# A four-layer graph network on one NeuronCore: narrower destination ranges, another sum over picked neighbours, another plan of picked passes

## The reference

```python
# layer 0: relational messages, weighted by an attention score of source, destination and relation
a   = tanh(relu(sum((x[src] @ A1.T + b1) * (x[dst] @ A2.T + b2 + rel_emb[etype])) / sqrt(32)))
nei = segment_sum(a * einsum('eb,ebo->eo', w_comp[etype], einsum('ei,bio->ebo', x[src], weight)), dst)
x = layernorm(x + relu(nei + x[src[last_edge]] @ self_loop_weight))      # nodes with an edge
x = layernorm(x + segment_sum(x[src], dst))                              # layer 1
x = layernorm(x + softmax_over_edges_weighted_sum(x[src]))               # layer 2, leaky-relu scores
x = layernorm(x + ten_steps_of_normalised_propagation(x))                # layer 3
```

## Time and profile before

| | |
|---|---|
| median of 3 runs | 1105.08 us |
| the profiled execution, its time | 1103.32 us |
| its span | 1101.10 us |
| busy in the span: VectorE, TensorE | 942.5 us (86%), 902.0 us (82%) |
| GpSimd, ScalarE | 579.0 us (53%), 533.2 us (48%) |
| indirect gathers | 534 |
| first and last duo, start of `products_of` | 74.58 us, 754.76 us |

### The profile page before, as it was taken

The page is one execution under the profiler, slowest core; times in us unless marked ns, Lnnn a source line. Parts: engine busy times, 40 slices in busy tenths (PEclk is TensorE's granted clock), DMA queues, the critical chain, the costliest instruction groups (busy, mean ns, idle before and its releaser), DMA issues.

```text
span 1101.1 us, 57074 instructions
## 1 busy us (share of the span) xinstructions
PE 902.0 (82%) x24130; PEld 846.5 (77%) x24130; DVE 942.5 (86%) x2309; ACT 533.2 (48%) x1342; POOL 579.0 (53%) x546
## 2 busy tenths in 40 slices
PE   3338888988988988888888888885849958999996
PEld 3327778877877887778788778775749958999996
DVE  7959999999999999999999999996469976555556
ACT  1126565655656567767767767777675300000000
POOL 5777777777777777777777777772000000000000
PEclk9559998989989989989989989996869979999998
DMA  5253232323323333333333333320000000000001
GB/s 121 45 88 59 53 68 59 60 55 69 57 54 62 63 57 59 64 62 59 60 68 57 58 65 59 67 43 8 5 1 4 4 2 4 4 4 4 5 4 19
DMA packets 54401, 48.55 MB, mean 44 GB/s; under 512 B 35470, under 2 KB 44142, under 8 KB 54142
## 3 DMA queue, kind: packets, MB, share of 16 engines
q0 software_dynamic: 17088, 8.78, 10.6%
q10 hardware_dynamic: 11456, 22.01, 6.0%
q1 hardware_dynamic: 25598, 14.07, 5.5%
HBM read 42.49 MB, written 2.32 MB: 41 GB/s over the span
## 4 chain that ended last, share of the span: by engine, by line
DVE 51%; PE 33%; issue 7%; ACT 5%; DMA 3%; ACTq 0%; SPq 0%; DVEq 0%
PE ps L885 14%; DVE arena L1418 11%; DVE arena L1385 11%; PE ps L818 4%; PE ps L932 3%; DVE aggT L1431 3%; DVE arena L1439 3%; DVE arena L1400 2%; DVE arena L1412 2%; DVE arena L1404 2%; DVE arena L1375 2%; PE ps L916 2%; DVE arena L1362 2%; DVE arena L1448 2%; PE ps L856 2%
## 5 line engine op out<-in xcount | busy, mean ns | idle before, releaser
L632 POOL DMA_INDIRECT arena<-x_pad,arena x534 | 577.1, 1081 | 163.0 <-issue 162.4
L818 PE MATMUL ps<-aggT 128*128 128x128 f16 x3472 | 226.5, 229 | 0.0
L818 PEld LDWEIGHTS ps<-aggT 128*128 128x128 f16 x3472 | 215.8, 104 | 2.1 <-DVE aggT L1431 0.4
L1385 DVE TENSOR_SCALAR arena<-pair_no,arena 128x275 bf16<-128x275 f16 (+2 forms) x784 | 183.5, 287 | 0.0
L885 PE MATMUL ps<-arena,adj_words 128*128 128x64 f16 x5625 | 171.9, 192 | 3.4 <-DVEq L1703 3.2
L885 PEld LDWEIGHTS ps<-arena,adj_words 128*128 128x128 fp8e4 x5625 | 170.5, 97 | 4.7 <-DVEq L1703 3.6
L1418 DVE TENSOR_TENSOR arena<-ps,arena 128x1536 f32<-128x1536 f32 x98 | 171.3, 1748 | 0.2
L1080 ACT ACTIVATE adj_words<-arena 128x500 uint8 x196 | 126.6, 646 | 56.8 <-ACT arena L1055 56.0
L1050 ACT ACTIVATE arena<-ps 128x500 fp8e4<-128x500 f32 x196 | 114.3, 583 | 56.3 <-PE ps L767 34.4
L780 PE MATMUL ps<-arena 128*32 128x44 f32 (+3 forms) x7048 | 133.0, 211 | 5.4 <-DVE arena L1418 5.1
L780 PEld LDWEIGHTS ps<-arena 128*32 128x32 f32 x7048 | 109.0, 112 | 26.4 <-DVE arena L1418 8.2
(11 more groups left out here) (223 smaller groups left out, 1152.0 us busy)
## 6 DMA issues: line engine op xcount, KB each, us to landing
arena<-line_table ACTq DMA_DIRECT2D x48, 344.0 KB
arena<-x_pad,arena POOLq DMA_INDIRECT x534
arena<-pick_table SPq DMA_DIRECT2D x31, 256.0 KB
arena<-line_table ACTq DMA_DIRECT2D x48, 80.0 KB
arena<-dst_parts SPq DMA_DIRECT2D x196, 5.7 KB
agg_table<-arena SPq DMA_DIRECT2D x196, 2.5 KB
dst_parts<-aggT ACTq DMA_DIRECT2D x1, 735.0 KB, 11.4
x<-x_pad ACTq DMA_DIRECT2D x1, 400.0 KB, 13.7
```

The costliest lines, as they stand in the source:

```text
L632: pool.indirect_dma_start(to, None, table, bass.IndirectOffsetOnAxis(ap=index, axis=0)).then_inc(done, 16)
L818: mm = nc.tensor.matmul(ps[:, at:at + PICK_WIDE * FEAT], pick_hot[:, u % PICK_RING, k * P:(k + 1) * P], x_parts[:, t, j * PICK_WIDE:(j + 1 ...
L1385: last = v.tensor_scalar(pair_hot[:, d % 2, k, 0:n], pair_no[:, 0:n], pair_of[:, d * DUO + k // SLOTS, k % SLOTS:k % SLOTS + 1], None, ALU ...
```

## The change

Four constants change, and what hangs on them: pages of 19 destinations for 20; ranges of 7, 9, 9 and 9 destinations for 8, 11, 11 and 11 (the last slot has one more column group for the carried destination: 10 for 12); starts 0, 2, 6, 10. The mixed values of a duo are 8 x 10 x 16 for 8 x 12 x 16. The products keep their number, with fewer columns. The plan of passes becomes three of (3, 2, 2) and one of (4, 3), so four passes take 11 duos and not 12: by `pick_plan` there are 34 passes for 31 (34, not 35), 238 units for 217, and 510 gathers for 534. The layout of `x_parts` and of the picked candidates puts the four candidates of a feature side by side, so one reduction (new L1448) replaces the two additions, and it is written behind `make_pairs(d + 1, 6, WIDE)`. The masks are made in 16 instructions for 4, `x_parts` in 8 for 2. Through `final_after`, which depends on `PAGE`, `count_piece` runs in duos 43 to 67 and 70 to 94, where before it ran in 46 to 70 and 72 to 96.

```diff
-PAGE = 20
-STARTS = (0, 1, 5, 9)
-WIDTH = 11
+PAGE = 19
+STARTS = (0, 2, 6, 10)
+WIDTH = 9
 HOTS = WIDTH + 1
-PAIR_DSTS = (8, WIDTH, WIDTH, HOTS)
+PAIR_DSTS = (7, WIDTH, WIDTH, HOTS)
...
-PICK_UNITS = ((3, 2, 2),)
+PICK_UNITS = ((3, 2, 2), (3, 2, 2), (3, 2, 2), (4, 3))
...
-        x_parts = pick.cut(2 * PICK_DEEP * PICK_WIDE * FEAT, F16).rearrange("p (t b f) -> p t b f", t=2, f=FEAT)
+        x_words = pick.cut(2 * PICK_DEEP * PICK_WIDE * FEAT, F16)
+        x_parts = x_words.rearrange("p (t j f w) -> p t j w f", t=2, f=FEAT, w=PICK_WIDE)
+        x_quad = x_words.rearrange("p (t j c) -> p t j c", t=2, c=FEAT * PICK_WIDE)
...
-                                                  x_parts[:, t, j * PICK_WIDE:(j + 1) * PICK_WIDE, :]
-                                                  .rearrange("p b f -> p (b f)"),
+                                                  x_quad[:, t, j, :],
...
-            link(v.memset(x_parts[:, :, BLOCKS:PICK_DEEP * PICK_WIDE, :], 0.0))
-            link(v.tensor_scalar(x_parts[:, 0, 0:BLOCKS, :], x[:], PICK_SCALE, None, ALU.mult))
-            link(v.scalar_tensor_tensor(out=x_parts[:, 1, 0:BLOCKS, :], in0=x[:], scalar=PICK_SCALE,
-                                        in1=x_parts[:, 0, 0:BLOCKS, :], op0=ALU.mult, op1=ALU.subtract))
+            link(v.memset(x_parts[:, :, PICK_DEEP - 1], 0.0))
+            for w in range(PICK_WIDE):
+                of = x[:, w::PICK_WIDE, :]
+                high, low = [x_parts[:, t, 0:-(-(BLOCKS - w) // PICK_WIDE), w, :] for t in range(2)]
+                link(v.tensor_scalar(high, of, PICK_SCALE, None, ALU.mult))
+                link(v.scalar_tensor_tensor(out=low, in0=of, scalar=PICK_SCALE, in1=high, op0=ALU.mult, op1=ALU.subtract))
...
-                def add_halves():
-                    half = PICK_WIDE // 2
+                def add_picked(c):
                     chain.wait()
                     dve.sem_inc(pick_read, 1)
-                    step(v.tensor_tensor(picked_of[:, :, 0:half], picked_of[:, :, 0:half], picked_of[:, :, half:PICK_WIDE], ALU.add))
-                def add_pairs(c):
-                    chain.wait()
-                    step(v.tensor_tensor(xp[:, PICKED[c] % AHEAD, :, 0:FEAT], picked_of[:, :, 0, :], picked_of[:, :, 1, :], ALU.add))
+                    step(v.tensor_reduce(xp[:, PICKED[c] % AHEAD, :, 0:FEAT],
+                                         picked.rearrange("p (k f w) -> p k f w", k=WIDE, w=PICK_WIDE), AX.X, ALU.add))
...
                     if more:
                         make_rows(d + 1)
-                    if picked_now is not None:
-                        add_halves()
                     if more:
                         make_pairs(d + 1, 6, WIDE)
                     if picked_now is not None:
-                        add_pairs(picked_now)
+                        add_picked(picked_now)
```

More of the change, by code:

```diff
@@ L1432, in make_pick_hot @@
                      .then_inc(pick_hots, 1)
-                picked_of = picked.rearrange("p (k w f) -> p k w f", k=WIDE, w=PICK_WIDE)
                 def mask_picked(c):
                     dve.wait_ge(pick_used, PICK_DEEP * (c + 1))
-                    n = [P, WIDE * PICK_WIDE, FEAT]
-                    step(v.tensor_tensor(picked.rearrange("p (w f) -> p w f", f=FEAT),
+                    n = [P, WIDE, FEAT, PICK_WIDE]
+                    step(v.tensor_tensor(picked.rearrange("p (k f w) -> p k f w", k=WIDE, w=PICK_WIDE),
                                          ps[:, PICK_AT_BANK:PICK_AT_BANK + WIDE * PICK_WIDE * FEAT]
-                                         .rearrange("p (w f) -> p w f", f=FEAT),
-                                         pick_mask[:, c].rearrange("p k w -> p (k w)").unsqueeze(2).to_broadcast(n), ALU.mult))
-                def add_halves():
-                    half = PICK_WIDE // 2
+                                         .rearrange("p (k f w) -> p k f w", k=WIDE, w=PICK_WIDE),
+                                         pick_mask[:, c].unsqueeze(2).to_broadcast(n), ALU.mult))
+                def add_picked(c):
                     chain.wait()
                     dve.sem_inc(pick_read, 1)
-                    step(v.tensor_tensor(picked_of[:, :, 0:half], picked_of[:, :, 0:half], picked_of[:, :, half:PICK_WIDE], ALU.add))
-                def add_pairs(c):
-                    chain.wait()
-                    step(v.tensor_tensor(xp[:, PICKED[c] % AHEAD, :, 0:FEAT], picked_of[:, :, 0, :], picked_of[:, :, 1, :], ALU.add))
+                    step(v.tensor_reduce(xp[:, PICKED[c] % AHEAD, :, 0:FEAT],
+                                         picked.rearrange("p (k f w) -> p k f w", k=WIDE, w=PICK_WIDE), AX.X, ALU.add))
                 make_lines(0)
```

## The result

The changed kernel takes **1256.74 us** (median of 4 runs, 1251.74 to 1257.64) against 1104.69 us for the kernel before: ratio 1.137, 95% interval 1.134 to 1.140, 152 us slower. I had forecast 1094 us.

A forecast was written before the change was run, and what follows sets the result against it. VectorE was taken to bound the sweep. Its work -15.9, the preparation +6.0 and the last wait -1.0 made -10.9 us: 1092.4 against the profiled 1103.32, so a median of 1094 us; 8-in-10 range 1084 to 1102.

The forecast's parts named there:

- Waits and the end: VectorE's waits in the sweep: earlier pairs and (4, 3) cycles cancel to 0; last duo's wait for ScalarE gives -1 us.
- ends of -8.5 and +17.6: Extremes for VectorE's waits: all 8.5 us ahead of the last duo vanish, or eight (4, 3) cycles add 17.6 us.
- VectorE's work: VectorE's instructions in the sweep: 37.4 us lost, 21.5 us gained, so 15.9 us less.
- the pairs: VectorE's 784 pair comparisons with fewer columns: 6.4 us less, with odd column counts costing 13 ns more.
- The ranges' work: VectorE's narrower mixed values, pair comparisons, `weigh` and `make_dst_hot` in the sweep: together 37.4 us less.
- the new plan's: Three more passes on VectorE, each with 7 code comparisons, a mask and a reduction: 15.3 us more.
- That the sum of the work is the time: In the sweep VectorE's own instructions set the pace; its time is their sum plus some 13 us.
- Without it VectorE could gain about 3 us before it ran into the gathers: GpSimd's queue in the sweep: without 24 fewer gathers (33 us less), VectorE could gain only about 3 us.
- The preparation: VectorE's masks and parts of `x` before the sweep, written at every fourth place: 6.0 us more, nothing hiding it.
- the rule of the Trainium skill: In the preparation, one-source operations keep two values a cycle whatever the step: about 1 us more, kernel about 1089 us.
- TensorE in the (4, 3) cycles: Rival: TensorE at low clock bounds these cycles, up to 17.6 us, 1112 us; chance 0.11 for part, 0.07 slower.
- The gathers: Rival: GpSimd's gathers set the sweep's pace, so 33 us would go, 1072 us; given nothing beyond the tail.

The follow-up runs named there:

- runs 8 and 1: Run 8 is `lines_split`, run 1 is `after_page18`.
- run 9: The changed kernel with pages of 18 rows and side and line loads of 20 rows: 1096.55 us, ratio 0.9922 to the kernel before.
- four cells: Narrow ranges, one sum; old plan 1092.39 us with the line load whole, 1077.55 split; new plan 1096.55 whole, 1099.49 split.
- run 10: The changed kernel with pages of 18, side and line loads of 20 rows and the old plan of passes: 1092.39 us, ratio 0.991.
- after_page18: The changed kernel with pages of 18 rows and starts 0, 2, 6, 9: 1097.66 us, ratio 0.9945 to the kernel before.
- lines_split: The changed kernel with the 86-row line load issued as 80 and 6 rows: 1100.90 us, ratio 0.9977 to the kernel before.

## Why the prediction was wrong

**The failed step is "Waits and the end".** It says "Two things change them", pair comparisons and the (4, 3) cycles, and lets them cancel, with ends of -8.5 and +17.6. Both are waits of VectorE on other compute engines. The third, SyncE's queue, was not in the sum, nor the rivals, nor the range. It had no entry because I read only VectorE's waits, where nothing behind the first lines waited for a load: that showed SyncE's lead in the kernel before, not that the change would leave it. The diff touches its side loads and stores: PAGE is their row count. The wait of 148.5 us on SyncE's queue was in the view before, and so was its pace, 3.66 us a group against VectorE's 3.51. What the runs showed in its place is a queue of 4.60 us a group, since 19 rows go through one DMA engine. Its size was 156 to 159 us (runs 8 and 1), nearly the whole miss of 163: without it the kernel stands at 1097 to 1101 us.

**VectorE's work: right, with the pairs sized low.** Mixed values 1480 ns (1482 costed), the reduction 1207 ns (1220), the mask unchanged. The ranges' work is 40.0 us by busy time with the split line load (942.8 before, 902.8 narrow; 37.4 costed), the new plan's 16.0 (914.6 to 930.6; 15.3 costed). Of the pairs, 225 columns took 286 ns (283 costed), but 250 took 288, no less than the 289 of 300; by these durations they saved 4.7 us for my 6.4. But durations of neighbours overlap, and the line's busy time, which counts an overlap once, fell by 11.0 us (14 ns for each of 784); by it, the pairs saved more than I costed. Before, then after:

```profile
L1385 DVE TENSOR_SCALAR arena<-pair_no,arena 128x275 bf16<-128x275 f16 (+2 forms) x784 | 183.5, 287 | 0.0
```
```profile
L1388 DVE TENSOR_SCALAR arena<-pair_no,arena 128x225 bf16<-128x225 f16 (+2 forms) x784 | 172.5, 281 | 0.0
```

The mean time from one comparison's start to the next one's, where two stand in a row, agrees: 218 ns for 275 columns and 192 for 225, 213 for 300 and 193 for 250, 181 for 200 and 175 for 175.

**That the sum of the work is the time: only in part.** For the whole change with spread DMAs it came near (-7.5 us for -10.9), and in part by luck. In run 9 VectorE's busy time fell by 12.2 us (942.5 to 930.3) for the 9.9 of the forecast, but the time from the first to the last `products_of` by 8.3 (680.2 to 671.9), where 17 was forecast: the mask's wait grew to 7.3 us and the wait for codes to 6.4, from 2.9 and none. The start of the first `products_of` rose by 4.5 us and not 6. For the parts it did not hold: the ranges gave 12.7 of 37.4 us. "Without it VectorE could gain about 3 us before it ran into the gathers" was the right mechanism; with the ranges alone and the line load split, the gathers stop it after some 11 us (1103.67 to 1092.41), since they became faster themselves (1081 to 1069 ns). The fewer gathers of the new plan are what it needs, unless the gathers get faster, which the one sum does by itself: hence 1077.55 us without the plan. Where the rest of the four cells' differences comes from (4 us for the plan with the line load whole, 22 with it split) is partly SyncE's queue, whose waits for codes are 18.3 us in run 10 and 6.4 in run 9; I did not separate it further.

**The preparation: right.** The masks took 303 and 278 ns (313 and 295 costed). Of the parts of `x`, those of 224 values took 649 and 656 ns and the second kind of 192 took 584 (0.65 and 0.58 us costed), but the first kind of 192 took 380, between the two prices. The rise was 5.2 us to the start of the sweep's first clearing (56.96 to 62.20 us), for my 6.0. The first mixed values started at 85.01 us, 7.2 later, since the wait for the first lines grew too, from 10.0 to 12.4 us. The row was the better guide than the rule of the Trainium skill, by which the rise would be about 1.

```profile
L1320 DVE TENSOR_SCALAR arena<-arena 128x72 f16<-128x72 int32 x8 | 2.4, 303 | 0.3
L1320 DVE TENSOR_SCALAR arena<-arena 128x64 f16<-128x64 int32 x8 | 2.2, 278 | 0.3
L1328 DVE SCALAR_TENSOR_TENSOR aggT<-x,aggT 128x192 f16<-128x192 f32 x3 | 1.8, 584 | 0.1
L1327 DVE TENSOR_SCALAR aggT<-x 128x192 f16<-128x192 f32 x3 | 1.1, 380 | 0.1
L1328 DVE SCALAR_TENSOR_TENSOR aggT<-x,aggT 128x224 f16<-128x224 f32 x1 | 0.7, 656 | 0.0
L1327 DVE TENSOR_SCALAR aggT<-x 128x224 f16<-128x224 f32 x1 | 0.6, 649 | 0.0
```

**The rivals.** TensorE in the (4, 3) cycles: the mask's wait is 9.9 us in 13 waits after, more than the 5 I had set, 6.7 in `after_page18` and 12.1 in `lines_split`; it exists and is small. The gathers: not in the change (in run 9 the last one starts at 695.4 us, 55.6 us before the last `products_of`), but in its ranges alone. None covered the result.

## What to carry to other kernels

A row count is a property of every DMA that is cut by it: before changing one, see on how many engines each of them lands, for instance by the packets of its queue, and whether a long transfer lives on the same ones. A queue on which nobody waits has a lead, not a zero cost: work out its time per turn against the pace of its reader, and how much it may grow. Here that was 3.66 against 3.51 us, from the trace of before alone. When one engine's gain is costed, name the next bound and its distance; here the queue and the gathers both stood some 12 us behind, and two ways to add that looked alike in cost (one sum, two additions) moved the gathers by 20.

## What the chip did that I had not expected

- 19 rows went through one DMA engine and 20 through ten. One engine took rows from two queues in turn, a row of 128 or 294 bytes for each of 4 KB (159 ns); a side load and a store of 19 rows then held SyncE for 6 to 7 us behind a line load. Splitting that load into 80 and 6 rows gave 156 us back.
- GpSimd's gathers had a mean of 1069 ns beside two f32 additions on VectorE and 1031 ns beside one reduction, over 534 of them (1060 and 1039 with the line load whole). The edit between them is the sum and its layout; which instruction slows them was not tried.
- Comparisons of 250 and 300 columns took 288 and 289 ns, 225 took 286 and 275 took 296, so by duration the width hardly counts; from start to start they took 193 and 213, 192 and 218 ns, so it does. Where neighbours overlap, durations mislead.
- A tensor_scalar that writes 16-bit values at every fourth place took 303 ns for 72 values (from int32), and 380 for 192 and 649 for 224 (from f32).
